# Base rows by channel batches, C and B by DMA, planes normalised in phase order, in a four-layer convolution kernel

## The chip, the cores and the metric

One core of a Trainium2 chip runs the whole program. The metric is the device time of one execution in microseconds (us), here as the median of several. PE, DVE, ACT and POOL are the compute engines; SP issues most DMAs. Work passes between engines by semaphores.

## What is computed

Four layers follow one another on x of shape 2 x 192 x 64 x 64; before each one the channels are normalised in groups of six, and its result is added to its input.

```python
# layer 0
base = conv1x1(x, w_qkv)                                    # 576 channels
qkv = concat(dw3x3(base), dw5x5(base), dw7x7(base))         # 1728 channels
qkv = conv1x1(qkv, w_pconv)                                 # channel attention on q, k, v, top-k softmax, w_proj
# layer 1: q, k, v = conv1x1(x, w_qkv); softmax(q k^T) v over channels, 8 heads
# layer 2: scan over 4096 positions, 192 channels, 16 states n
h = exp(d_t * A) * h + (d_t * x_t) * B_t[n]
y_t = sum_n h[n] * C_t[n] + x_t * D                         # then W_out
# layer 3: depthwise 7 x 7 convolution and a bias
```

## The kernel before

Channels lie on partitions in `NT` = 3 tiles: tile 0 and 1 hold channels 0 to 127 of either image, tile 2 holds channels 128 to 191 of both, 64 partitions each (`pieces`). `mem` is the one SBUF arena, `ps` the one PSUM tensor, so these names stand in nearly every row of the profile.

**Layer 0, depthwise.** `layer0_depthwise` has 36 batches n of 16 base channels. The rows of an image are sorted by phase: 56 rows (`TAPROWS`) on partitions, so that a depthwise convolution becomes matmuls with tap matrices. The 1x1 product gives the base for 128 channels m at a time, in eight groups g; ACT and DVE split it into high and low fp16 parts (`base`), POOL shifts six groups by a column (`shift`), and SP stores both to `base_phases` in DRAM (`store_base` L405, `store_shifted` L413). m = 0 is done ahead; m + 1 is done in the first four batches of each eight, two groups a batch. For a batch, SP loads windows from `base_phases` (`load_windows` L425, two DMAs, to partitions 0 to 55 and 64 to 119) and taps from `in_wd` (`load_taps` L399, also two). ACT copies the taps to fp16 (`taps`, L535, L538), POOL takes the low part (`split_taps`, L579, L582), PE runs four units of 36 matmuls (L500), each copied out by ACT (L545) and split by DVE (L606), and SP stores the 96 rows (`store_out` L431, three DMAs of 32 partitions). SP's order in a batch is: outputs of n - 1, windows of n + 2, taps of n + 2, base stores. There are three window buffers and two tap buffers.

**Layer 2.** `layer2` first makes delta, B and C by products; B and C in three bf16 parts are moved between partitions by 24 SBUF-to-SBUF DMAs. The scan then runs for t in three tiles, j in four chunks of 1024 positions, n in 16 states, 192 steps in all. For a step: PE spreads row B[n] over the partitions with a selector matmul (`b_bcast`, L1526), ACT makes the decay (L1593), DVE multiplies (L1665) and scans (L1679), PE spreads C[n] to PSUM (`c_bcast`, L1535), ACT copies it to `cs` (L1599), POOL multiplies h by it (L1650), PE adds over states (`accumulate`, L1551). For the four `POOL_STATES` the B row goes by PE (L1542) and ACT (L1602) to POOL, which makes the product (L1647) in place of DVE. ACT also keeps the last column of h (L1579).

**Layer 3.** `layer3` normalises each tile, splits it into fp16 high and low parts in phase order, mirrors columns and rows at the borders, and stores planes to DRAM, 4 MB for tile 0 and 1 and twice 2 MB for tile 2. ACT makes the high part from the natural layout (L1854), DVE the normalised tile (L1924) and the low part (L1928) and the columns (L1931, L1932); POOL makes two shifted copies (L1894, L1895) and the low part of the taps (L1888); then DVE copies the mirrored rows (`rows(t)`, L1912, L1914), which SP's store (L1794) waits for. Then 12 steps load patches (L1808, four DMAs), multiply (L1841), copy out (ACT L1872) and store to `conv_d` (L1876); SP loads the sums back by channel (L1818), DVE adds (L1946), SP stores the result (L1822).

## Time and profile before

| | us |
|---|---|
| median of 3 runs | 2782.25 |
| lowest and highest | 2777.99, 2783.22 |
| the profiled execution | 2779.78 |
| its span, first to last instruction | 2777.9 |

| stretch, us | work |
|---|---|
| 94 to 627 | batches of layer 0's depthwise part |
| 1731 to 2476 | the 192 scan steps of layer 2 |
| 2542 to 2778 | layer 3 after its norm |

Times in rows are us unless marked ns. The DMA share is the busy share of the core's 16 DMA engines. A transfer that is issued waits behind those issued earlier on its queue.

### The profile page before, as it was taken

Reading aid. Unit: us, or ns where it says so; the run is one execution under the profiler, and the core shown is the slowest. Engines: PE = TensorE matmul, PEld = TensorE weight load, DVE = VectorE, ACT = ScalarE, POOL = GpSimd, SP = SyncE. Lnnn points to the kernel's source line nnn. Section 1 sums busy time; section 2 is a strip of 40 time slices with the busy share of each in tenths; the row PEclk is TensorE's granted clock in tenths of the full one; section 3 lists DMA queues with packets and bytes.
Section 4 is the critical chain, followed back from the end, with each engine's and each line's share of the span. In section 5 each row is a group of like instructions: output and inputs, shape, how many; then the busy total and the mean of one; then the engine's idle time right before and its main releaser. Section 6 shows DMA issues by size and latency. Waiting matters only on the chain. (4 is left out here: it accounts for less than half of the span.)

```text
span 2777.9 us, 38167 instructions
## 1 busy us (share of the span) xinstructions
PE 2059.9 (74%) x16032; PEld 1257.4 (45%) x16032; DVE 1303.1 (47%) x1197; ACT 1022.2 (37%) x1444; POOL 849.1 (31%) x446
## 2 busy tenths in 40 slices
PE   3768787767999999999489658777678678772032
PEld 1466665665777777777235222222223223221021
DVE  5334344341011010111450265798889799979703
ACT  2344444440000000000132236667676766655110
POOL 1333323220000000000000120687688678873300
PEclk9989898878999999999699779899899899996555
DMA  5899999987331331310300041000000000013399
GB/s 167 256 270 279 247 309 233 271 228 210 93 107 57 104 107 54 107 54 1 96 3 7 7 134 23 0 0 0 0 1 0 0 0 0 0 50 93 142 226 279
DMA packets 157448, 292.93 MB, mean 105 GB/s; under 512 B 10284, under 2 KB 135212, under 8 KB 151084
## 3 DMA queue, kind: packets, MB, share of 16 engines
q1 hardware_dynamic: 144620, 284.39, 36.1%
q10 hardware_dynamic: 12672, 6.29, 0.8%
q8 instruction: 118, 1.93, 0.3%
q14 instruction: 38, 0.31, 0.0%
HBM read 168.16 MB, written 120.91 MB: 104 GB/s over the span
## 5 line engine op out<-in xcount | busy, mean ns | idle before, releaser
L675 PE MATMUL ps<-mem 128*128 128x288 f16 x5376 | 653.9, 287 | 19.5 <-DMA mem<-depthwise_out 19.5
L675 PEld LDWEIGHTS ps<-mem 128*128 128x128 f16 x5376 | 501.8, 98 | 157.5 <-DMA mem<-depthwise_out 19.7
L1650 POOL TENSOR_TENSOR mem<-mem 128x1024 f32<-128x1024 f32 x192 | 460.6, 2412 | 86.1 <-ACT mem L1579 85.7
L1551 PE MATMUL ps<-mem 128*128 128x512 f32 x768 | 388.2, 630 | 12.9 <-POOL mem L1650 12.1
L500 PE MATMUL ps<-mem 56*96 56x240 f16 (+1 forms) x5184 | 311.8, 282 | 107.6 <-DVE mem L606 98.3
L1679 DVE TENSOR_TENSOR_SCAN mem<-mem,ps 128x1024 f32<-128x1024 f32 x144 | 335.8, 2332 | 89.7 <-issue 50.7
L500 PEld LDWEIGHTS ps<-mem 56*96 56x96 f16 x5184 | 300.5, 130 | 133.9 <-DVE mem L606 106.0
L1072 POOL TENSOR_TENSOR mem<-mem 128x1536 f16<-128x1536 f32 x16 | 50.8, 3179 | 996.3 <-ACT mem L1052 996.3
L715 DVE TENSOR_TENSOR mem<-mem 128x384 f32<-128x384 f32 x64 | 35.7, 559 | 610.8 <-ACT mem L729 610.8
L606 DVE TENSOR_TENSOR mem<-ps,mem 96x1024 f16<-96x1024 f32 x144 | 171.2, 1216 | 225.2 <-ACT mem L545 224.0
L727 ACT COPY mem<-ps 128x288 f32<-128x288 f32 x64 | 25.5, 398 | 645.7 <-PE ps L675 645.7
L1599 ACT COPY mem<-ps 128x1024 f32<-128x1024 f32 x192 | 194.1, 1011 | 121.3 <-PE ps L1535 78.4
L1551 PEld LDWEIGHTS ps<-mem 128*128 128x128 f32 x768 | 148.3, 199 | 160.0 <-issue 102.3
L545 ACT CAST mem<-ps 96x1024 f16<-96x1024 f32 x144 | 140.1, 1007 | 103.9 <-PE ps L500 103.9
L1526 PE MATMUL ps<-mem 96*128 (+1 forms) x288 | 91.1, 405 | 117.1 <-DVE mem L1679 110.1
L1665 DVE TENSOR_TENSOR ps<-ps,mem 128x1024 f32<-128x1024 f32 x144 | 174.2, 1209 | 2.4 <-PE ps L1526 2.4
L1647 POOL TENSOR_TENSOR mem<-mem 128x1024 f32<-128x1024 f32 x48 | 115.7, 2410 | 165.4 <-ACT mem L1602 165.3
L1593 ACT ACTIVATE mem<-mem 128x1024 f32<-128x1024 f32 (+1 forms) x144 | 165.5, 1150 | 1.4 <-issue 1.1
L579 POOL TENSOR_TENSOR mem<-mem 120x768 f16<-120x768 f32 x36 | 62.0, 1722 | 326.9 <-ACT mem L538 326.9
L1841 PE MATMUL ps<-mem 56*32 56x256 f16 x1728 | 43.9, 378 | 157.6 <-DMA mem<-l_planes 127.3
L1535 PE MATMUL ps<-mem 96*128 (+1 forms) x384 | 120.2, 396 | 53.3 <-ACT mem L1602 53.3
L481 PE MATMUL ps<-mem 128*128 128x512 f32 (+1 forms) x160 | 92.4, 707 | 43.2 <-DVE mem L600 26.7
(204 smaller groups left out, 2119.0 us busy)
## 6 DMA issues: line engine op xcount, KB each, us to landing
depthwise_out<-mem SPq DMA_DIRECT2D x108, 512.0 KB, 8.1
mem<-depthwise_out SPq DMA_DIRECT2D x32, 1664.0 KB, 9.9
mem<-base_phases SPq DMA_DIRECT2D x72, 448.0 KB
base_phases<-mem SPq DMA_DIRECT2D x56, 512.0 KB, 9.6
mem<-in_wd SPq DMA_DIRECT2D x72, 336.0 KB
mem<-l_planes SPq DMA_DIRECT2D x48, 252.0 KB
mem<-in_x SPq DMA_DIRECT2D x4, 2048.0 KB, 11.0
l_planes<-mem SPq DMA_DIRECT2D x2, 4032.0 KB, 13.3
```

Of the source, the lines that this page charges most:

```text
L500: ins = nc.tensor.matmul(out.rearrange("p (b n) -> p b n", b=B)[:, :, lo:hi], wh[n % 2][p, c0:c0 + MD], x, start=(o == 1 and i == 0), stop ...
L545: nc.scalar.copy(stg_part(n, k, 0), dw_psum(u)).then_inc(dw_hi, 1)
L606: nc.vector.tensor_tensor(stg_part(n, k, 1), dw_psum(u), stg_part(n, k, 0), ALU.subtract).then_inc(dw_lo, 1)
L675: ins = nc.tensor.matmul(ps[:, 2 * (i % 2) + h, 0:HALF], d, pw[rows, wa, k, HALF * h:HALF * h + HALF], start=(k == 0 and n == 0), stop=(k ...
L1535: ins = nc.tensor.matmul(pc[:, a, :], sel[0:96, N * t + n, :], bc3[0:96, 1, bass.ds(j * CH + 512 * a, 512)], start=True, stop=True)
L1551: ins = nc.tensor.matmul(py[:, a, :], ident, hh[:, n % 4, 512 * a:512 * a + 512], start=(n % N == 0), stop=(n % N == N - 1))
L1593: nc.scalar.activation(decay, halves(zs[t][:, bass.ds(j * CH, CH)]), ACT.Exp, scale=na[:, t, n:n + 1]).then_inc(exp_done, 1)
L1599: nc.scalar.copy(halves(cs[:, n % 2, :]), pc).then_inc(c_copied, 1)
L1647: nc.gpsimd.tensor_tensor(dbx, dbx, dxs[t % 2][:, bass.ds(j * CH, CH)], ALU.mult).then_inc(dbx_pool, 1)
L1650: nc.gpsimd.tensor_tensor(hh[:, n % 4, :], hh[:, n % 4, :], cs[:, n % 2, :], ALU.mult).then_inc(hc_pool, 1)
L1665: V.tensor_tensor(pb[n % 2], pb[n % 2], halves(dxs[t % 2][:, bass.ds(j * CH, CH)]), ALU.mult).then_inc(dbx_done, 1)
L1679: V.tensor_tensor_scan(hh[:, n % 4, :], decay, drive, 0.0 if first else hs[:, n:n + 1], ALU.mult, ALU.add).then_inc(scan_done, 1)
```

## The change

**Layer 0.** `base_phases` in DRAM is laid out by phase row, then channel, where it was channel, then row. A window load then reads 8 KB in one run for each partition (eight neighbouring channels) where it read eight runs of 1 KB (every other channel); a base store writes four runs of 1 KB for each partition where it wrote one of 4 KB. `stg_part` and the tap layout follow the new pairing of channels. There are three tap buffers, `load_taps` runs three batches ahead, and ACT converts the taps of n + 1 after unit 1 of batch n, where it did so ahead of unit 0.

```diff
-        base_d = nc.dram_tensor("base_phases", [QKV, TAPROWS, PITCH0], F16).ap()
+        base_d = nc.dram_tensor("base_phases", [TAPROWS, QKV, PITCH0], F16).ap()
...
-    NM, NSTB, NWIN, NSTG = 5, 4, 3, 3
-    w = ar.take(2, QKV)
+    NM, NSTB, NWIN, NSTG, NTB = 5, 4, 3, 3, 3
+    w = spare.rearrange("p a c -> p (a c)").rearrange("p (a c) -> p a c", a=2)
...
-    w32 = [ar.take(BP * TAPS0) for _ in range(2)]
+    w32 = [ar.take(BP * TAPS0) for _ in range(NTB)]
...
 
-        return stg[n % NSTG][0:MD, 4 * k:4 * k + 4, 256 * a:256 * a + 256].rearrange("p (q t) n -> p t q n", t=2)
...
-                    sp.dma_start(base_d[128 * m:128 * m + width(m), row:row + 4, :].rearrange("c r n -> c (r n)"),
-                                 ext[0:width(m), SHIFTED.index(g)].rearrange("p r n -> p (r n)")).then_inc(ext_stored[SHIFTED.index(g)], 16)
+                    sp.dma_start(base_d[row:row + 4, 128 * m:128 * m + width(m)].rearrange("r c n -> c r n"),
+                                 ext[0:width(m), SHIFTED.index(g)]).then_inc(ext_stored[SHIFTED.index(g)], 16)
...
-                    sp.dma_start(win[64 * t:64 * t + TAPROWS, slot], base_d[c0 + t:c0 + 2 * BP:2].rearrange("c f n -> f c n")
-                                 ).then_inc(win_loaded[slot], 16)
+                    sp.dma_start(win[64 * t:64 * t + TAPROWS, slot], base_d[:, c0 + BP * t:c0 + BP * t + BP]).then_inc(win_loaded[slot], 16)
...
@@ -452,9 +451,10 @@
                     if (n + 2) % BP == 0:
                         wait_stored((n + 2) // BP)
                     load_windows(n + 2)
+                if n + NTB < NBATCH:
                     sp.wait_ge(w_lo, NTAP * (n + 1))
                     sp.wait_ge(w_hi, NTAP * (n + 1))
-                    load_taps(n + 2)
+                    load_taps(n + NTB)
...
-                if n + 1 < NBATCH:
-                    taps(n + 1)
                 for k in range(UPB):
                     for m, g in base_before(n, k):
                         base(m, g)
                     unit(n, k)
+                    if k == 1 and n + 1 < NBATCH:
+                        taps(n + 1)
```

ACT in two batches that make no base; L545 is a unit's copy, L535 and L538 are the taps of the next batch. Before:

```order
L535 CAST mem<-mem 120x8x96 [waits l0_depthwise_in_psum_54,l0_taps_loaded_48]
L538 CAST mem<-mem 120x8x2x8
L538 CAST mem<-mem 120x8x2x16
L538 CAST mem<-mem 120x8x2x24
L545 CAST mem<-ps 96x2x2x256 [waits l0_depthwise_stored_58,l0_depthwise_in_psum_54]
L545 CAST mem<-ps 96x2x2x256 [waits l0_depthwise_in_psum_54] x3
```

Now:

```order
L545 CAST mem<-ps 96x2x2x256 [waits l0_depthwise_stored_59,l0_depthwise_in_psum_55]
L545 CAST mem<-ps 96x2x2x256 [waits l0_depthwise_in_psum_55]
L535 CAST mem<-mem 120x8x96 [waits l0_depthwise_in_psum_55,l0_taps_loaded_49]
L538 CAST mem<-mem 120x8x2x8
L538 CAST mem<-mem 120x8x2x16
L538 CAST mem<-mem 120x8x2x24
L545 CAST mem<-ps 96x2x2x256 [waits l0_depthwise_in_psum_55] x2
```

The four conversions stand behind two units of a batch, and the unit copies of the same batch that stood behind them are ahead.

**Layer 2.** B and C are stored in fp32 to DRAM (`bc_d`) during the products, and half of the SBUF moves go. For each step SP loads the row C[n] from there into one of four slots of `cs`, as two DMAs that each repeat one 4 KB row on 64 partitions; for a state of `POOL_STATES` it does the same for B into one of two slots of `dbx`. PE's `c_bcast` and `pool_b_bcast` and ACT's two copies are gone. The products split B and C through a new tile, so that the unsplit values can be stored.

```diff
+            for k in range(NK2):
+                sp.wait_ge(bc_out, k + 1)
+                for b in range(B):
+                    sp.dma_start(bc_d[b, :, 512 * k:512 * k + 512], full[64 * b:64 * b + 2 * N_STATE, k % 2]).then_inc(bc_stored[k % 2], 16)
+                if k % 4 == 3:
+                    s = slice(512 * (k - 3), 512 * (k + 1))
+                    sp.wait_ge(bcv, 5 * (k + 1))
+                    for part in range(3):
+                        for b in range(B):
+                            sp.dma_start(b3[32 * part + 16 * b:32 * part + 16 * b + 16, s],
+                                         parts[64 * b:64 * b + 16, part, s]).then_inc(moved, 16)
...
+                for h in range(2):
+                    b = t if t < 2 else h
+                    sp.dma_start(dst[64 * h:64 * h + 64], bc_d[b, row, j * CH:j * CH + CH].partition_broadcast(64)).then_inc(done, 16)
+
+            def load_b(m):
+                t, j, n = m // (N * NCH), m // N % NCH, m % N
+                if pool_count(t, j, n) > 2:
+                    sp.wait_ge(scan_done, m - 8 + 3)
+                spread(dbx[:, pool_slot(n)], n, t, j, b_loaded[pool_slot(n)])
+
+            load_b(POOL_STATES[0])
+            for m in range(N * NCH * NT):
+                t, j, n = m // (N * NCH), m // N % NCH, m % N
+                if m + 4 < N * NCH * NT and (m + 4) % N in POOL_STATES:
+                    load_b(m + 4)
+                if m >= 4:
+                    sp.wait_ge(hc_pool, m - 4 + N + 1)
+                spread(cs[:, n % 4], N + n, t, j, c_loaded[n % 4])
+
         @block.tensor
         def _(pe):
             def b_bcast(t, j, n):
                 pe.wait_ge(scan_done, count(t, j, n) + 1)
...
-            def c_bcast(t, j, n):
-                pe.wait_ge(c_copied, count(t, j, n) + 1)
-                if n - 1 in [q - 2 for q in POOL_STATES]:
-                    pe.wait_ge(b_copied, pool_count(t, j, n + 1))
-                for a in range(2):
-                    ins = nc.tensor.matmul(pc[:, a, :], sel[0:96, N * t + n, :], bc3[0:96, 1, bass.ds(j * CH + 512 * a, 512)],
-                                           start=True, stop=True)
-                ins.then_inc(csum, 1)
...
-                    c_bcast(t, j, n)
                     if n >= 2 or not first:
                         accumulate(t, j, n - 2)
-                    if n + 2 in POOL_STATES:
-                        pool_b_bcast(t, j, n + 2)
...
-                    act.wait_ge(csum, count(t, j, n) + 1)
-                    wait_times_c(act, t, j, n - 2)
-                    nc.scalar.copy(halves(cs[:, n % 2, :]), pc).then_inc(c_copied, 1)
-                    if n + 2 in POOL_STATES:
-                        act.wait_ge(bsum_pool, pool_count(t, j, n + 2))
-                        nc.scalar.copy(halves(dbx), pc).then_inc(b_copied, 1)
...
-                            pool.wait_ge(b_copied, pool_count(t, j, n + 2))
-                            nc.gpsimd.tensor_tensor(dbx, dbx, dxs[t % 2][:, bass.ds(j * CH, CH)], ALU.mult).then_inc(dbx_pool, 1)
+                            db = dbx[:, pool_slot(n + 2)]
+                            pool.wait_ge(b_loaded[pool_slot(n + 2)], 32 * ((pool_count(t, j, n + 2) + 1) // 2))
+                            nc.gpsimd.tensor_tensor(db, db, dxs[t % 2][:, bass.ds(j * CH, CH)], ALU.mult).then_inc(dbx_pool, 1)
                         pool.wait_ge(carried, m + 3)
-                        pool.wait_ge(c_copied, m + 2)
-                        nc.gpsimd.tensor_tensor(hh[:, n % 4, :], hh[:, n % 4, :], cs[:, n % 2, :], ALU.mult).then_inc(hc_pool, 1)
+                        pool.wait_ge(c_loaded[n % 4], 32 * (m // 4 + 1))
+                        nc.gpsimd.tensor_tensor(hh[:, n % 4, :], hh[:, n % 4, :], cs[:, n % 4, :], ALU.mult).then_inc(hc_pool, 1)
```

ACT in the first chunk of a scan; L1593 (now L1606) is the decay, L1579 (L1592) the kept column, L1583 (L1596) the skip term. Before:

```order
L1593 ACTIVATE mem<-mem 128x1024 [waits l2_scan_120]
L1579 COPY mem<-mem 128x1 [waits l2_scan_120]
L1599 COPY mem<-ps 128x1024 [waits l2_h_times_c_121,l2_c_broadcast_114]
L1602 COPY mem<-ps 128x1024 [waits l2_pool_b_broadcast_118]
L1583 ACTIVATE mem<-mem 128x2048 [waits l2_dx_ready_111]
L1593 ACTIVATE mem<-mem 128x1024 [waits l2_scan_120]
L1579 COPY mem<-mem 128x1 [waits l2_scan_120]
```

Now:

```order
L1606 ACTIVATE mem<-mem 128x1024 [waits l2_scan_126]
L1592 COPY mem<-mem 128x1 [waits l2_scan_126]
L1596 ACTIVATE mem<-mem 128x2048 [waits l2_dx_ready_114]
L1606 ACTIVATE mem<-mem 128x1024 [waits l2_scan_126]
L1592 COPY mem<-mem 128x1 [waits l2_scan_126]
```

The copies L1599 and L1602 between the decays are gone.

**Layer 3.** ACT alone normalises, a quarter r at a time, into `tmp` in phase order; DVE copies that to the high part and subtracts it for the low part. One shifted copy moves from POOL to ACT, the other to DVE, and `rows(t)` follows its own tile's columns. The first taps load during the norm. `stg` has four slots and shares memory with `tmp`. The result is added and stored in halves. Some semaphores are layer 0's again, with their counts as a base.

```diff
-            for i in range(NPIECE):
-                if i >= 2:
-                    sp.wait_ge(tap_hi, i - 1)
-                    sp.wait_ge(tap_lo, i - 1)
-                sp.dma_start(w32[i % 2][0:64 + TAPROWS], inp["wd3"][:, 3 * WC * i:3 * WC * (i + 1)]).then_inc(tap_in[i % 2], 16)
             for t in range(NT):
+                if t < 2:
+                    sp.wait_ge(tap_hi, t + 1)
+                    sp.wait_ge(tap_lo, t + 1)
+                    load_taps(sp, t + 2)
                 sp.wait_ge(rows_done, t + 1)
...
+            for k in range(NSTG):
+                sp.wait_ge(conv_stored[k], 32 * (128 // CB // NSTG))
             sp.wait_ge(stored[2], 32)
...
+                for h in range(2):
+                    s = slice(HW // 2 * h, HW // 2 * (h + 1))
+                    sp.wait_ge(added, 8 * t + 4 * h + 4)
+                    for p0, b, c0, n in pieces(t):
+                        sp.dma_start(xout[b, c0:c0 + n, s], xt[p0:p0 + n, t, s]).then_inc(out_stored, 16)
...
+            def normalise(t):
                 for r in range(4):
-                    nc.scalar.activation(flat(main_rows(t, r, 0)), natural(xt[:, t], r), ACT.Identity,
-                                         bias=nb[:, t:t + 1], scale=rs[:, t:t + 1]).then_inc(x_hi, 1)
+                    if t:
+                        act.wait_ge(x_lo, 4 * t - 3 + r)
+                    nc.scalar.activation(phase_rows(r).rearrange("p f (y x) -> p f y x", x=8), natural(xt[:, t], r), ACT.Identity,
+                                         bias=nb[:, t:t + 1], scale=rs[:, t:t + 1]).then_inc(x_norm, 1)
...
-            split(0)
+            def shift_right(t):
+                k = t % 2
+                act.wait_ge(x_lo, 4 * (t + 1))
+                nc.scalar.copy(grid(pl[:, k, 8:11])[:, :, :, 1:8], grid(pl[:, k, 5:8])[:, :, :, 0:7]).then_inc(shifted, 1)
+
+            normalise(0)
             taps(0)
-            split(1)
-            taps(1)
-            split(2)
-            taps(2)
-            taps(3)
+            for t in range(NT):
+                shift_right(t)
+                if t + 1 < NT:
+                    normalise(t + 1)
+                taps(t + 1)
...
+                if n >= NSTG:
+                    act.wait_ge(conv_stored[n % NSTG], 32 * (n // NSTG))
...
-            for t in range(NT):
-                pool.wait_ge(x_lo, 4 * (t + 1))
-                pool.wait_ge(x_hi, 4 * (t + 1))
-                k = t % 2
-                nc.gpsimd.tensor_copy(grid(pl[:, k, 8:11])[:, :, :, 1:8], grid(pl[:, k, 5:8])[:, :, :, 0:7]).then_inc(shifted, 1)
-                nc.gpsimd.tensor_copy(grid(pl[:, k, 11:14])[:, :, :, 0:7], grid(pl[:, k, 0:3])[:, :, :, 1:8]).then_inc(shifted, 1)
-                taps(t)
-            taps(3)
+            for i in range(NPIECE):
+                taps(i)
...
+                if t == 2:
+                    dve.wait_ge(stored[0], 16)
                 for r in range(4):
+                    dve.wait_ge(x_norm, 4 * t + r + 1)
+                    V.tensor_copy(main_rows(t, r, 0), phase_rows(r)).then_inc(x_hi, 1)
                     dve.wait_ge(x_hi, 4 * t + r + 1)
-                    V.tensor_tensor(flat(main_rows(t, r, 1)), natural(tmp, r), flat(main_rows(t, r, 0)), ALU.subtract).then_inc(x_lo, 1)
+                    V.tensor_tensor(main_rows(t, r, 1), phase_rows(r), main_rows(t, r, 0), ALU.subtract).then_inc(x_lo, 1)
                 dve.wait_ge(x_lo, 4 * t + 4)
+                V.tensor_copy(grid(pl[:, k, 11:14])[:, :, :, 0:7], grid(pl[:, k, 0:3])[:, :, :, 1:8]).then_inc(shifted, 1)
                 for i in range(3):
                     V.tensor_copy(column(k, 8 + i, 0), column(k, 3 - i, 0)).then_inc(columns, 1)
                     V.tensor_copy(column(k, 11 + i, 7), column(k, 6 - i, 7)).then_inc(columns, 1)
-                if t:
-                    rows(t - 1)
-            rows(NT - 1)
+                rows(t)
...
+                dve.wait_ge(conv_in[t], conv_base[t] + 16 * len(pieces(t)))
+                for h in range(2):
+                    for r in range(4):
+                        x = natural(xt[:, t], r)[:, :, 8 * h:8 * h + 8]
```

DVE in layer 3 where the second tile ends. L1912 and L1914 before are the rows of the first tile, and L1924, L1928 the third tile. Before:

```order
L1932 COPY mem<-mem 128x8x16
L1912 COPY mem<-mem 128x14x2x8 x3
L1914 COPY mem<-mem 128x14x2x8 x3
L1924 TENSOR_SCALAR mem<-mem 128x4096
L1928 TENSOR_TENSOR mem<-mem 128x8x128 x4
L1931 COPY mem<-mem 128x8x16
```

Now (L1955, L1956 are columns, L1935 and L1937 rows, L1953 the shifted copy, L1949 and L1951 the high and low part), where the first tile ends and the second begins:

```order
L1955 COPY mem<-mem 128x8x16
L1956 COPY mem<-mem 128x8x16
L1935 COPY mem<-mem 128x14x2x8 x3
L1937 COPY mem<-mem 128x14x2x8 x3
L1949 CAST mem<-mem 128x8x128
L1951 TENSOR_TENSOR mem<-mem 128x8x128
```

The rows of a tile stand right behind its columns, where they stood behind the whole next tile.

## Rows read from the trace of the kernel before

**Rows 1.** Stretches (from:to, length, busy us of each engine, clock, DMA share, GB/s).

```profile
94.00:627.00 533.00, 409.74 (x5424) 330.85 (x5422) 217.33 (x207) 234.04 (x343) 160.51 (x159) 0.88 0.96 263
```

**Rows 2.** Waits of 90 to 650 us: who for whom, total us, times, longest.

```profile
ACT mem L535 <- DMA mem<-in_wd: 161.4, 33, 10.9
...
PE ps L500 <- DVE mem L606: 98.3, 21, 9.7
```

**Rows 3.** Stretches in which one kind of transfer moves almost alone.

```profile
4.00:12.00 8.00, 0.00 (x0) 0.00 (x0) 2.84 (x5) 0.00 (x0) 0.00 (x0) 1.00 1.01 430
13.00:21.00 8.00, 0.00 (x0) 0.00 (x0) 5.85 (x10) 0.00 (x0) 0.00 (x0) 1.00 0.95 199
574.00:578.00 4.00, 4.00 (x77) 4.00 (x79) 1.22 (x1) 0.67 (x1) 0.00 (x0) 1.00 0.94 199
...
1605.00:1608.00 3.00, 3.00 (x22) 1.06 (x22) 2.17 (x4) 0.16 (x1) 2.76 (x1) 1.00 0.96 367
...
2502.00:2504.00 2.00, 0.94 (x4) 0.42 (x5) 2.00 (x2) 0.40 (x1) 0.96 (x1) 0.96 0.96 246
```

**Rows 4.** DMA of 735 to 740 us, 1 KB packets to 128 partitions.

```profile
DMA packets 1714, 1.71 MB, mean 341 GB/s; under 512 B 48, under 2 KB 1714, under 8 KB 1714
```

**Rows 5.** DMA issues of the page: count, KB of one, us to landing.

```profile
mem<-base_phases SPq DMA_DIRECT2D x72, 448.0 KB
base_phases<-mem SPq DMA_DIRECT2D x56, 512.0 KB, 9.6
...
mem<-l_planes SPq DMA_DIRECT2D x48, 252.0 KB
```

**Rows 6.** Groups of instructions, 1731 to 2476 us: busy us, mean ns, idle before, releasers.

```profile
L1650 POOL TENSOR_TENSOR mem<-mem 128x1024 f32<-128x1024 f32 x192 | 460.6, 2412 | 86.1 <-ACT mem L1579 85.7
L1551 PE MATMUL ps<-mem 128*128 128x512 f32 x768 | 388.2, 630 | 12.9 <-POOL mem L1650 12.1 <-DVE mem L1684 0.6
L1679 DVE TENSOR_TENSOR_SCAN mem<-mem,ps 128x1024 f32<-128x1024 f32 x144 | 335.8, 2332 | 89.7 <-issue 50.7 <-ACT mem L1593 19.5 <-DVE ps L1665 17.3
L1599 ACT COPY mem<-ps 128x1024 f32<-128x1024 f32 x192 | 194.1, 1011 | 121.3 <-PE ps L1535 78.4 <-POOL mem L1650 42.8
L1665 DVE TENSOR_TENSOR ps<-ps,mem 128x1024 f32<-128x1024 f32 x144 | 174.2, 1209 | 2.4 <-PE ps L1526 2.4
...
L1647 POOL TENSOR_TENSOR mem<-mem 128x1024 f32<-128x1024 f32 x48 | 115.7, 2410 | 165.4 <-ACT mem L1602 165.3
```

**Rows 7.** Timeline at one state of `POOL_STATES`: start, us, engine, line.

```profile
2015.12 1.01 ACT L1602 COPY mem<-ps 128x1024 f32<-128x1024 f32 x1 [1.14 <-PE ps L1542]
...
2016.03 1.15 ACT L1593 ACTIVATE mem<-mem 128x1024 f32<-128x1024 f32 x1
...
2017.27 2.29 DVE L1679 TENSOR_TENSOR_SCAN mem<-mem,ps 128x1024 f32<-128x1024 f32 x1 [0.86 <-DVE ps L1665]
```

**Rows 8.** Stretches: the scans as a whole, and their first 60 us.

```profile
1731.00:2476.00 745.00, 564.34 (x1535) 213.38 (x1532) 647.39 (x359) 508.38 (x652) 574.75 (x240) 0.94 0.00 0
1731.00:1791.00 60.00, 41.13 (x99) 15.16 (x96) 43.59 (x25) 42.05 (x49) 35.18 (x15) 0.79 0.00 0
```

**Rows 9.** Timeline of layer 3, in order of time.

```profile
2558.81 4.60 DVE L1932 COPY mem<-mem 128x128 f16<-128x128 f16 x1
...
2585.16 44.20 SPq L1794 DMA_DIRECT2D l_planes<-mem  x4
2600.67 8.58 ACT L1854 ACTIVATE mem<-mem 128x1024 f16<-128x1024 f32 x4 [36.89 <-DMA l_planes<-mem]
...
2626.96 0.47 DVE L1914 COPY mem<-mem 128x224 f16<-128x224 f16 x3
...
2637.87 84.52 SPq L1808 DMA_DIRECT2D mem<-l_planes  x48
...
2663.93 3.95 PE L1841 MATMUL ps<-mem 56*32 56x256 f16 x144 [125.16 <-DMA mem<-l_planes]
```

**Rows 10.** Waits of 2530 to 2778 us.

```profile
ACT mem L1872 <- DMA l_conv<-mem: 13.7, 2, 8.4
```

145 lines of the change are left out of this document (66 added, 79 removed).

## The prediction

> **What bounds the kernel now.** I read the busy shares by stretch first, since the three changed places have different limits, then in each stretch what is waited for.
>
> In layer 0's depthwise part, 94 to 627 us, the DMA engines are busy for 0.96 of 533 us and PE for 410 us [rows 1]. ACT waits 161 us in total for taps, and PE 98 us for a PSUM bank that frees late, behind ACT [rows 2]. That looks like a stall to be removed, but while ACT waits, the DMA engines are moving the bytes it waits for: only the 0.04 left, 21 us, is idle DMA time. So transfers set this stretch. What a transfer costs depends on the partitions it touches: 128 partitions go at 430 GB/s, and 64 partitions, in the same kind of load, at 199; 56 partitions in 1 KB runs (the windows) at 199 too; 4 KB runs are stored from tiles of mostly 128 partitions at 367 [rows 3]. 1 KB runs to 128 partitions go at 341 [rows 4].
>
> In the scans, 1731 to 2476 us, nearly no DMA runs. DVE is busy for 647 of 745 us, POOL 575, PE 564, ACT 508 [rows 8]. DVE's idle time stands almost wholly before the scans, 89.7 us [rows 6]. One place shows why: ACT copies B from PSUM (L1602) from 2015.12 on, so its decay (L1593), which starts at 2016.03, ends only at 2017.18, and DVE's scan starts at 2017.27, 0.86 us late [rows 7]; the row names DVE as the releaser, but its product had ended. In the first 60 us DVE is busy for only 43.6 [rows 8]. DVE is the bound, and ACT's copies are what makes it late.
>
> In layer 3 a chain of preparations ends in the stores of the planes and the patch loads behind them. The third tile's high part starts at 2600.67, after the first store has landed, and the rows of the second and third tile follow only at the end, up to 2627.4 (three copies of 0.47 us in the row); the patch loads are issued at 2637.87 and PE starts at 2663.93, after 125 us of waiting for patches [rows 9].
>
> **Layer 0, part by part.** Windows: 72 loads of 448 KB [rows 5], 0.92 MB a batch. At the 199 GB/s of the row they take 4.6 us, and as runs of 8 KB they still go to 56 partitions, so I take half of 430, 215 GB/s, 4.3 us: 36 x 0.34 = 12 us less DMA time. Bounds: nothing, and 36 x 2.5 = 89 us less at 430, which I exclude because large runs to 64 partitions stayed at 199. Base stores: 56 of 512 KB [rows 5] and 14 of half that, 63 units. A unit takes 1.43 us at 367 GB/s and 1.54 at 341, so +0.11 each, 7 us; the other bound is the windows' own 199, 2.63 us, +76 us. I take the near one, +9 with some margin, since these stores use 128 partitions. Taps three ahead and converted mid-batch move the same bytes, one batch's earlier; they could give back the 21 us of idle DMA time. Against it: POOL now splits the taps mid-batch, and its shifts of the base rows, queued behind, come later, and SP's store of the shifted rows, and behind that the outputs of the next batch, wait for them. I take 5 us back. How late are the taps of n + 1? In all, a batch costs ACT 234 / 36 = 6.5 us, with four unit copies and its share of the base, and POOL 160.5 / 36 = 4.5, with the shifts [rows 1]; so I put the conversion at some 2 us and the split under 4.5, together 6 after unit 1, while PE's other two units take half of its 410 / 36 = 11.4, 5.7 us with base products among them, 4 without. PE would wait up to 2 us a batch, which hides while the DMAs set a batch at 533 / 36 = 14.8 us, and costs if they stop doing so. Sum for layer 0: -12 + 9 - 5 = -8 us, bounds -35 and +65.
>
> **Layer 2, part by part.** PE loses the 384 matmuls of `c_bcast` and the 96 for POOL's B, ACT loses 192 copies of 1.011 us [rows 6] and 48 more, 243 us of its 508. The decays can then run as far ahead as the PSUM bank and the scan two steps back let them, so I let the waits before scans go by two thirds: 0.65 x 89.7 = 58 us. Not more, because POOL is near: four steps cost it 5 x 2.41 = 12.1 us, and DVE 3 x (2.33 + 1.21) + 2.3 = 12.9 [rows 6]. The new transfers: four steps need ten DMAs of 256 KB, 2.6 MB. Every one touches 64 partitions: at 246 GB/s (4 KB runs, half of the partitions [rows 3]) that is 10.7 us, at 199 it is 13.2 us, which would set the pace. I take up to 12, between them and nearer to the first, whose runs are of the same 4 KB: just hidden beneath DVE's 12.9, with four slots of C, about 13 us, to cover a late one. No row shows one DRAM row read 64 times over; its bounds are these rates and a rival below. SP issues some 480 DMAs and does nothing else here. If the cover is gone, each 1 us more for four steps costs 48 us. The stores of B and C and the 12 moves fewer lie beside the products; costed at nothing. Bounds for the scans: -78 and -20 (POOL and the transfers in turn late), catastrophes apart.
>
> The Trainium skill, "DMA: Bandwidth & Descriptors", section "Anatomy of one DMA — SWDGE (gpsimd) path", fits 2.0 us plus bytes / 436 GB/s for a single DMA (of another queue than SP's). By that, one after the other, ten DMAs of 256 KB take 26 us for four steps, and the scans 48 x 26 = 1250 us. The sum by the rule would be 1250 - 687 = 563 us slower than mine. The row speaks against it: 48 patch loads of 252 KB are issued in 84.5 us, 1.8 us each with conv stores among them [rows 5, 9], so queued DMAs overlap their fixed part. I go by the row; what it leaves of the rule is rival F.
>
> **Layer 3, part by part.** ACT's quarter takes 8.58 / 4 = 2.15 us [rows 9] as before. DVE's pair in place of normalising and subtracting I put at 0.9 + 1.2 us: the second is the 1209 ns of the same size in [rows 6], the first, an unseen cast, lies between 0.5 and 1.2. So a tile takes some 9 us, then the shifted copy some 2, six columns at 0.47, 3, and the rows 1. A DVE copy beside POOL's tap subtraction waits it out (4.60 us for one small copy, where others take 0.47, [rows 9]); I add that once a tile. From 2542 to the store of tile 0 are thus 20 us: 2563, and then 2583 and 2603. Before, the first was at 2585.16 and the last after 2627.4 [rows 9]. The first store has landed by 2575, ahead of the third tile's need. Patch loads then stand only behind tile 2's 4 MB from 64 partitions, 19 us at half rate, and not behind tile 1's as well: 2663.9 becomes about 2631, -32 us. Bounds -22 and -38. The twelve steps stay at their DMA pace. At the end ACT waits 13.7 us for stores of its two stage slots [rows 10], queued against SP's loads; with four slots the last sums are stored earlier and tile 2's load follows: -6 us, bounds 0 and -12. Halved adds save little, as the outputs wait for each other on the DMA engines.
>
> **Sum.** -8 - 58 - 32 - 6 = -104 us. The profiled execution took 2779.8, so 2675.8; it lies inside the three runs, 2.5 us under their median, and I leave the forecast at 2676.
>
> **Rivals.**
>
> A, slower: the repeated row. All 16 DMA engines read the same 4 KB 64 times, then again for the other half. If that halves the rate of 246 GB/s to 123, four steps take 21.3 us, the scans 48 x 21.3 = 1022 us and the whole 2676 + 335 = 3011. It decides from the rate at which four steps take more than 745 / 48 + 46 / 48 = 16.5 us, 159 GB/s, where all that the other parts gain is eaten. For it: no row shows such a load. Against it: nothing in the rows slows with the source, only with the partitions reached. Chance 0.08.
>
> The Trainium skill, "SBUF — State Buffer", section "A bandwidth-pool intuition that's wrong (but worth ruling out)", gives about 22.5 GB/s for one of 32 HBM ports. Were a 4 KB row behind one port, four steps would take 116 us and the scans over 5 ms; no run here shows how rows spread, and this is the far end of A.
>
> B: the scans are paced by POOL and the transfers together, 15.1 us for four steps (12.1 of POOL and 3 of waiting for loads): scans 725 us, total 2676 + 38 = 2714. For it: 12.1, 12 and 12.9 us are close. Chance 0.14.
>
> C: the base stores in 1 KB runs go at the windows' rate: +76 in place of +9, total 2743. For it: they share engines with windows. Against it: 341 GB/s with 128 partitions. Chance 0.07.
>
> D: the taps were more than a symptom: with bigger runs and earlier taps PE's waits of 98 us [rows 2] halve as well, 41 us more than I gave, with the stretch down to 484 us, total 2676 - 41 = 2635. For it: transfers that PE's waits delay would go with them. Against it: 0.96 of 533 us is 512 us of DMA work, which would have to shrink by more than the 12. Chance 0.13.
>
> E: PE's clock. Less PE work in the scans; in their first 60 us PE was busy for 41 and the granted clock 0.79 against 0.94 over all [rows 8], between 1.2 and 2.4 GHz. If it stayed low, `accumulate`, four times 0.63 us at mostly full clock [rows 6], and B would pass DVE's 3.5 us a step; the scans 100 us longer than now forecast, the total 2776, within 0.2% of before. Chance 0.03.
>
> F: transfers that cost what the patch loads cost, 84.5 / 48 = 1.76 us for 252 KB [rows 5, 9], whatever the reason. Ten take 17.6 us for four steps, the scans 845 us, 158 more than forecast, total 2834. It decides above the same 16.5 us as A. For it: the size is the same. Against it: conv stores from few partitions share those 84.5 us. Chance 0.02.
>
> The forecast itself has 0.53.
>
> **How the numbers follow.** The forecast's own spread runs from 2640 to 2710. B adds up to 2714 to 2730, D down to 2630. The range 2628 to 2735 leaves out A, E, F, C's upper half and the ends of D, 0.2 together. A measurement can tell 0.2%, 5.6 us. Faster by more: forecast, B, C, D, 0.87, less 0.01 for their ends. Within: part of E, 0.02. Slower: A, F and the worse half of E, 0.12.
>
> **What would show it.** In the profile after: DMA share near 0.97 in layer 0 and a stretch of 515 to 540 us; ACT no longer waiting for taps at the head of a batch. In the scans a DMA share around 0.8 to 0.95, the idle time before scans under 35 us, ACT under 300 us busy, POOL's waits on loads small. In layer 3 the first store of planes 21 us after the start of the stage (2563 against 2542, where it was 43), all three within 42 us, and 27 to 30 us from the last to PE's start. It is wrong if POOL waits long for the loads of C (A or B), if the base stores' windows show under 300 GB/s (C), or if layer 0 is shorter by over 30 us (D).

## The result, and the profile after

| | before | after |
|---|---|---|
| median, us | 2782.73 | 2617.67 |
| lowest and highest | 2777.99, 2785.88 | 2613.45, 2630.39 |
| profiled execution, span | 2779.78, 2777.9 | 2617.27, 2615.5 |

The ratio is 0.9416, with a 95% interval of 0.9381 to 0.9451: 165 us less, where 104 was forecast and the range's lower end was 2628. By stage, from the two traces:

| stage | before | after | difference | forecast |
|---|---|---|---|---|
| layer 0, first to last depthwise matmul | 534.0 | 471.2 | -62.8 | -8 |
| layer 2, first to last scan | 736.0 | 672.2 | -63.8 | -58 |
| layer 3, last scan to the end | 307.8 | 272.0 | -35.8 | -38 |
| all else | 1200.1 | 1200.1 | 0.0 | 0 |

Two of the three terms held. Layer 0 gave 55 us more than it was priced at, and the excess of the total over the forecast, 58 us, is nearly all there.

Three stretches of after (columns as in [rows 1]): layer 0's batches, four of them with base products, and the scans.

```profile
92.00:563.00 471.00, 393.86 (x5432) 324.31 (x5428) 222.08 (x207) 239.93 (x348) 162.11 (x164) 0.92 0.96 297
...
410.00:450.00 40.00, 40.00 (x480) 26.15 (x476) 22.33 (x24) 23.32 (x36) 17.05 (x16) 1.00 0.98 294
1671.00:2344.00 673.00, 492.97 (x1047) 186.24 (x1048) 642.54 (x357) 281.08 (x409) 575.74 (x240) 0.87 0.74 186
```

The first row answers to [rows 1]: the DMA share is 0.96 as before, but the same bytes now go at 297 GB/s where they went at 263, and PE's busy time of 394 us fills 84% of the stage in place of 77%. In the second row PE is busy for 40.00 of 40 us while the DMA share is 0.98: a share near one stands beside a PE that never waits. The third row answers to [rows 8]: DVE is busy for 643 of 673 us, ACT for 281 where it had 508, the DMA share is 0.74, and the granted clock has gone from 0.94 to 0.87.

Waits of after, 88 to 580 us (as [rows 2]):

```profile
PE ps L500 <- DMA mem<-base_phases: 59.4, 9, 11.3
...
PE ps L500 <- DVE mem L606: 10.2, 3, 6.7
```

ACT's 161 us for taps are gone from this list, and PE's 98 us for a bank that DVE frees (L606) are 10. What is left is 59 us for windows.

Groups of after in the scans (as [rows 6]):

```profile
L1687 DVE TENSOR_TENSOR_SCAN mem<-mem,ps 128x1024 f32<-128x1024 f32 x144 | 335.8, 2332 | 26.6 <-issue 9.0 <-ACT mem L1606 8.7 <-ACT ps L1606 3.5
L1673 DVE TENSOR_TENSOR ps<-ps,mem 128x1024 f32<-128x1024 f32 x144 | 174.1, 1209 | 3.4 <-PE ps L1558 3.3
```

DVE's idle time before its scans is 26.6 us in place of 89.7. Its own instructions take what they took, 2332 and 1209 ns. With 643 of 673 us busy, DVE has little left to give back.

Timeline of after in layer 3 (as [rows 9]):

```profile
2416.50 8.64 ACT L1882 ACTIVATE mem<-mem 128x1024 f32<-128x1024 f32 x4 [1.93 <-PEq L203]
...
2435.44 0.35 SPq L1822 DMA_DIRECT2D l_planes<-mem  x1
...
2451.17 22.77 SPq L1822 DMA_DIRECT2D l_planes<-mem  x3
...
2474.12 91.50 SPq L1836 DMA_DIRECT2D mem<-l_planes  x48
...
2501.45 3.83 PE L1871 MATMUL ps<-mem 56*32 56x256 f16 x136 [88.12 <-DMA mem<-l_planes]
```

ACT starts to normalise at 2416.50, and the first store of planes is issued 19 us later, at 2435.44; the last is issued before 2474.12, when the patch loads begin, and PE starts 27 us after that. The forecast had 20 or 21 us, and 27 to 30.

### The profile page after: what moved, and what is told of

The parts are those of the page before. It is cut to its first block and busy times, and to the rows that moved or that the text cites. A ratio compares the mean times of both kernels' runs of the same rounds, so it can differ in the third digit from the quotient of the medians.

```text
span 2615.5 us, 37175 instructions
## 1 busy us (share of the span) xinstructions
PE 1977.8 (76%) x15552; PEld 1225.0 (47%) x15552; DVE 1291.3 (49%) x1222; ACT 808.9 (31%) x1207; POOL 835.6 (32%) x440
## 5 line engine op out<-in xcount | busy, mean ns | idle before, releaser
L1567 PE MATMUL ps<-mem 128*128 128x512 f32 x768 | 429.6, 691 | 23.3 <-POOL mem L1658 19.0
L1687 DVE TENSOR_TENSOR_SCAN mem<-mem,ps 128x1024 f32<-128x1024 f32 x144 | 335.8, 2332 | 26.6 <-issue 9.0
L606 DVE TENSOR_TENSOR mem<-ps,mem 96x1024 f16<-96x1024 f32 x144 | 175.4, 1220 | 219.2 <-ACT mem L545 219.2
L1567 PEld LDWEIGHTS ps<-mem 128*128 128x128 f32 x768 | 163.5, 221 | 222.0 <-issue 127.0
L1558 PE MATMUL ps<-mem 96*128 (+1 forms) x288 | 99.5, 436 | 162.6 <-DVE mem L1687 160.0
L545 ACT CAST mem<-ps 96x1024 f16<-96x1024 f32 x144 | 144.9, 1008 | 191.0 <-PE ps L500 191.0
L1673 DVE TENSOR_TENSOR ps<-ps,mem 128x1024 f32<-128x1024 f32 x144 | 174.1, 1209 | 3.4 <-PE ps L1558 3.3
L1606 ACT ACTIVATE mem<-mem 128x1024 f32<-128x1024 f32 (+1 forms) x144 | 163.5, 1143 | 1.3 <-issue 1.0
L1592 ACT COPY mem<-mem 128x1 f32<-128x1 f32 x192 | 36.6, 191 | 390.4 <-DVE mem L1687 390.4
L1558 PEld LDWEIGHTS ps<-mem 96*128 96x128 bf16 x288 | 23.8, 105 | 273.6 <-DVE mem L1687 234.9
L1687 DVE TENSOR_TENSOR_SCAN mem<-ps,mem 128x1024 f32<-128x1024 f32 x48 | 111.1, 2314 | 0.0
```

Source lines behind the costliest of these rows:

```text
L545: nc.scalar.copy(stg_part(n, k, 0), dw_psum(u)).then_inc(dw_hi, 1)
L606: nc.vector.tensor_tensor(stg_part(n, k, 1), dw_psum(u), stg_part(n, k, 0), ALU.subtract).then_inc(dw_lo, 1)
L1558: ins = nc.tensor.matmul(pb[n % 2][:, a, :], sel[0:96, N * t + n, :], b3[0:96, bass.ds(j * CH + 512 * a, 512)], start=True, stop=True)
L1567: ins = nc.tensor.matmul(py[:, a, :], ident, hh[:, n % 4, 512 * a:512 * a + 512], start=(n % N == 0), stop=(n % N == N - 1))
L1606: nc.scalar.activation(decay, halves(zs[t][:, bass.ds(j * CH, CH)]), ACT.Exp, scale=na[:, t, n:n + 1]).then_inc(exp_done, 1)
L1673: V.tensor_tensor(pb[n % 2], pb[n % 2], halves(dxs[t % 2][:, bass.ds(j * CH, CH)]), ALU.mult).then_inc(dbx_done, 1)
```

## The experiments

Each edit is made to the changed kernel, if not said otherwise. "Stage" is layer 0 from the first to the last depthwise matmul. Eight profiles in which layer 0's code is that of the change have stages of 471 to 482 us, and where the scans' code is untouched too they take 670 to 672 us; so differences of up to 11 us count as nothing in layer 0, and of 2 in the scans.

| run | edit | median, us | ratio | stage | scans |
|---|---|---|---|---|---|
| the change | | 2617.7 | 0.942 | 471 | 672 |
| `e1_old_taps` | two tap buffers, conversion ahead of unit 0 | 2671.2 | 0.959 | 530 | 672 |
| `e2_old_rows` | old row layout | 2617.8 | 0.941 | 470 | 672 |
| `e3_head` | three buffers, conversion ahead of unit 0 | 2606.6 | 0.936 | 463 | 672 |
| `e4_two_buffers` | two buffers, conversion mid-batch | 2649.2 | 0.950 | 510 | 672 |
| `e5_taps_first` | `e1_old_taps`, taps first in SP's order | 2586.0 | 0.928 | 447 | 670 |
| `b1_before_first` | the kernel before, taps first | 2690.8 | 0.966 | 437 | 733 |
| `o6_first_old_rows` | `e5_taps_first`, old row layout | 2585.5 | 0.929 | 443 | 670 |
| `o7_first_three` | the same, three buffers | 2586.5 | 0.929 | 448 | 672 |
| `o2_spread_base` | base steps over six batches | 2613.7 | 0.939 | 474 | 672 |
| `o1_two_queues` | upper partitions on ACT's queue | 2638.0 | 0.947 | 498 | 672 |
| `c1_more_bytes` | `e3_head`, 344 KB more a batch | 2650.9 | 0.952 | 501 | 672 |
| `s1_all_partitions` | loads of C and B to 128 partitions | 2619.3 | 0.941 | 476 | 672 |
| `s2_act_copies` | one more ACT copy a step | 2627.5 | 0.943 | 473 | 679 |
| `s4_copies_that_wait` | and it waits for POOL | 2627.3 | 0.943 | 476 | 682 |
| `s5_both_and_wait` | and a second copy, for 48 states | 2629.6 | 0.944 | 474 | 686 |
| `s6_c_by_pe` | C by PE and ACT again | 2652.1 | | 477 | 707 |
| `s7_b_by_pe` | POOL's B by PE and ACT again | 2680.3 | | 473 | 738 |
| `l3_both` | rows a tile later, two stage slots | 2632.1 | | 482 | 672 |

Where no ratio stands there was one execution, and only its trace is read.

### Layer 0: layout or timing of the taps

Edit of `e1_old_taps`:

```diff
-    NM, NSTB, NWIN, NSTG, NTB = 5, 4, 3, 3, 3
+    NM, NSTB, NWIN, NSTG, NTB = 5, 4, 3, 3, 2
...
+                if n + 1 < NBATCH:
+                    taps(n + 1)
                 for k in range(UPB):
...
-                    if k == 1 and n + 1 < NBATCH:
-                        taps(n + 1)
```

> The changed kernel with layer 0's taps as before: two tap buffers, loads two batches ahead, ACT converting the taps of n + 1 ahead of unit 0. The new row layout stays. In the changed kernel layer 0's stage (first to last depthwise matmul) takes 471 us, against 534 before. Theory 'rows' (the 8 KB window runs alone bring the gain): 471 to 480 us, total 2618 to 2627. Theory 'timing' (the taps' timing brings most of the 63 us): 505 to 525 us, total 2650 to 2670. If both carry a share, some 490, total 2637.

The stage is 530 us: the timing of the taps carries 59 of the 63. The stretch and two waits of this run:

```profile
92.00:622.00 530.00, 414.11 (x5432) 336.26 (x5432) 218.16 (x207) 234.60 (x343) 158.73 (x159) 0.88 0.94 265
```

```profile
ACT mem L535 <- DMA mem<-in_wd: 155.9, 33, 10.0
...
PE ps L500 <- DVE mem L606: 95.4, 18, 9.4
```

Both waits are those of before, 161 and 98 us, within 6 us. The new layout alone moved the stage from 534 to 530, less than the 11 us by which it varies.

Edit of `e2_old_rows` (and the base stores accordingly):

```diff
-        base_d = nc.dram_tensor("base_phases", [TAPROWS, QKV, PITCH0], F16).ap()
+        base_d = nc.dram_tensor("base_phases", [QKV, TAPROWS, PITCH0], F16).ap()
...
-                    sp.dma_start(win[64 * t:64 * t + TAPROWS, slot], base_d[:, c0 + BP * t:c0 + BP * t + BP]).then_inc(win_loaded[slot], 16)
+                    sp.dma_start(win[64 * t:64 * t + TAPROWS, slot], base_d[c0 + BP * t:c0 + BP * t + BP].rearrange("c f n -> f c n")).then_inc(win_loaded[slot], 16)
```

> The changed kernel with base_phases by channel, then row, as before: windows in 1 KB runs, base stores in 4 KB runs; three tap buffers and mid-batch conversion stay. Theory 'rows': layer 0 at 520 to 535 us, total 2667 to 2680. Theory 'timing': 475 to 490 us, total 2622 to 2637. If each carries a share alone, the two deficits of this run and of the one with old taps add up to 63 us; if either needs the other, they add up to more.

Stage and total are those of the change. So no run shows a worth of the layout, with late taps (4 us) or with taps in time (0). The two deficits, 59 and 0, add up to 63 but for what the stage varies by.

### Which half of the timing

`e3_head` puts the conversion back ahead of unit 0 and keeps three buffers; `e4_two_buffers` has two buffers and keeps the conversion mid-batch: the two halves of the first diff above.

> The changed kernel with three tap buffers and loads three batches ahead, but ACT converts the taps of n + 1 ahead of unit 0 of batch n, as before. With both the depth and the place of before, layer 0's stage took 530 us; with both changed, 471. Theory 'late transfer' (the taps arrive late because their load could not be issued earlier): depth alone brings it, stage 471 to 485 us, total 2618 to 2632. Theory 'place' (ACT's wait stands ahead of unit copies that could go): 515 to 530 us, total 2660 to 2675.

> The changed kernel with two tap buffers and loads two batches ahead, as before, but ACT converting the taps of n + 1 after unit 1 of batch n. Theory 'place': stage 471 to 485 us, total 2618 to 2632. Theory 'late transfer': 515 to 530 us, total 2660 to 2675. If each alone does nearly all, both runs stand near 2620: half a batch of slack in either form would have been enough.

The third buffer alone does all of it. It stands 8 us below both together (463 us against 471), which the stage's variation could make; the totals, 2606.6 and 2617.7, point the same way, with ratio intervals that just touch (up to 0.9387, from 0.9381). The place alone gives 20 of the 59. Mid-batch conversion seems to cost something beside three buffers, since PE then waits for the late split: 18.7 us for POOL (L582) in the trace of after, a wait that `e3_head` doesn't show. The prediction had feared up to 2 us a batch for it.

### Why the taps were late

Edit of `e5_taps_first`, on top of `e1_old_taps`:

```diff
             for n in range(NBATCH):
+                if n + NTB < NBATCH:
+                    sp.wait_ge(w_lo, NTAP * (n + 1))
+                    sp.wait_ge(w_hi, NTAP * (n + 1))
+                    load_taps(n + NTB)
                 if n >= 1:
                     store_out(n - 1)
...
                     load_windows(n + 2)
-                if n + NTB < NBATCH:
-                    sp.wait_ge(w_lo, NTAP * (n + 1))
-                    sp.wait_ge(w_hi, NTAP * (n + 1))
-                    load_taps(n + NTB)
```

> The changed kernel with layer 0's taps as before (two buffers, conversion ahead of unit 0, stage 530 us in that form), but SP issues the load of the taps of n + 2 first in batch n, ahead of its wait for the outputs of n - 1 and of the windows, where it stood behind both. Same bytes. Theory 'round trip' (the taps are late because their load stands behind the outputs' and windows' transfers in SP's order, and ACT's wait for them then holds up the next outputs): stage 465 to 490 us, total 2608 to 2630. Rival 'amount' (transfers as a whole set the stage with two buffers, in any order): 520 to 535 us, total 2660 to 2675.

Two buffers, the old place of the conversion, the same bytes, and only four lines of SP's program moved: 447 us, less than with the change's three buffers. The load was late since SP issued it behind `store_out(n - 1)`, which waits until the whole batch n - 1 is computed, and behind the outputs and windows themselves, 2.5 MB a batch. The edit takes it out from behind both; which of the two weighs more was not separated. The same edit in the kernel before:

> The kernel before, with one edit: SP issues layer 0's load of the taps of n + 2 first in batch n, ahead of the stores of outputs n - 1 and the windows. Theory 'round trip' (the late taps, not the bytes, set the stage): the stage falls from 534 us to 445 to 480, total 2695 to 2730. Rival (the gain of the run with the taps first needed the new layout or the new later stages): 515 to 534 us, total over 2765.

The stage falls from 534 to 437 us, the total to 2690.8, a ratio of 0.966 with an interval of 0.964 to 0.969. One moved load gives 97 us, more than all that the change does to layer 0. SP's own wait for outputs shrinks with it, to 12.2 us in 7 waits; in the kernel before, over the stage, it is:

```profile
SPq L431 <- DVE mem L606: 132.2, 34, 9.6
```

The round trip can be read in the kernel before, around batch 15 (timeline: start, us, engine, line; in brackets the idle time before and who ended it):

```profile
306.70 2.96 SPq L431 DMA_DIRECT2D depthwise_out<-mem  x3
...
310.03 3.95 SPq L425 DMA_DIRECT2D mem<-base_phases  x2
...
314.08 1.04 SPq L399 DMA_DIRECT2D mem<-in_wd  x2
...
324.12 0.83 ACT L535 CAST mem<-mem 120x768 f16<-120x768 f32 x1 [9.26 <-DMA mem<-in_wd]
...
325.78 2.81 ACT L545 CAST mem<-ps 96x1024 f16<-96x1024 f32 x3
...
328.09 3.91 PE L500 MATMUL ps<-mem 56*96 56x256 f16 x36 [8.61 <-DVE mem L606]
```

The outputs of n - 1 are stored at 306.70, as soon as they exist, windows follow at 310.03 and taps at 314.08. These taps land ten microseconds later, at 324.1, where ACT has waited 9.26 us for them; three finished units stand behind that wait in ACT's order, so PE waits 8.61 us for a bank. And the next outputs, the next loads behind them, and so the next taps, start later by as much. In the same kernel with the taps first:

```profile
310.64 2.64 SPq L399 DMA_DIRECT2D mem<-in_wd  x2
...
313.33 3.10 SPq L431 DMA_DIRECT2D depthwise_out<-mem  x3
...
316.48 4.86 SPq L425 DMA_DIRECT2D mem<-base_phases  x2
...
320.41 0.83 ACT L536 CAST mem<-mem 120x768 f16<-120x768 f32 x1
...
322.27 3.94 PE L501 MATMUL ps<-mem 56*96 56x256 f16 x72
```

Here the taps (310.64) go ahead of the outputs (313.33) and windows (316.48), and ACT converts taps at 320.41 without a wait. The two stretches are not quite alike: here the batches also make base products, so that PE has more to do while the loads run. In batches without base this run has waits for taps too (5.87 us at 253.30); over the stage there are 15 of them, where there were 33. The stretch and the waits of this run:

```profile
94.00:531.00 437.00, 385.73 (x5432) 315.01 (x5430) 220.33 (x207) 237.67 (x344) 162.42 (x159) 0.95 0.99 322
```

```profile
ACT mem L536 <- DMA mem<-in_wd: 45.7, 15, 9.0
...
PE ps L501 <- DVE mem L607: 32.6, 12, 6.1
```

The share is 0.99, higher than before, and the rate is 322 GB/s where it was 263, with packets of the same sizes: counted in the two traces over these stretches, a 16 KB packet of an output store takes 904 ns on average before and 749 here, a 6 KB packet of taps 394 and 308, a 1 KB packet of windows 74 and 61, and a 4 KB packet of a base store 169 and 170. The traces give a hint why. Before, 42% of the window packets ran while at least nine in ten packets under way were of their own size, and took 77 ns each; here 11% do, at the same 77 ns. But the others fell as well, from 72 to 59 ns, so this is not all of it. The wait for taps is 46 us in place of 161.

### What bounds layer 0 now

Edit of `c1_more_bytes`, on top of `e3_head`:

```diff
+                if n:
+                    sp.wait_ge(win_loaded[(n - 1) % NWIN], 64 * ((n - 1) // NWIN + 1))
+                for t in range(2):
+                    sp.dma_start(more[64 * t:64 * t + TAPROWS], base_d[:, c0:c0 + 3]).then_inc(win_loaded[slot], 16)
```

> The kernel with three tap buffers and the conversion at the head (stage 463 us, total 2607), with 344 KB more to load in each of the 36 batches, from base_phases in 3 KB runs to the windows' partitions, into a place that nobody reads; PE waits for it as for the windows. At the windows' 199 GB/s this is 1.7 us a batch, 62 us in all. Theory 'transfers set the stage' (their share is 0.97): 510 to 530 us. Rival 'PE sets it' (most batches take PE's own 13.5 or 10.5 us): 463 to 475 us. Between the two: only the batches that wait for windows grow, 480 to 500 us.

```profile
94.00:595.00 501.00, 405.93 (x5432) 333.45 (x5428) 220.92 (x207) 238.80 (x344) 164.90 (x159) 0.89 0.97 303
```

```profile
SPq L430 <- DMA mem<-base_phases: 72.4, 17, 14.4
```

The second row is SP's wait for the windows and added loads of the batch before, which the edit brings with it. The stage is 501 us, 38 more, about 0.6 of the 62 us that the bytes were priced at: with 12 MB more and a share of 0.97 again, the rate is 303 GB/s, as it was 301 without them. That doesn't show that the amount counts, though. SP stands 72.4 us in the added wait, which `e3_head` doesn't have, with the taps and the outputs behind it in SP's order. Bytes and lateness are not told apart by this run, and what bounds the stage of 471 us stays open: PE fills 84% of it and waits 59 us for windows. The share alone says the same in all these runs.

> The changed kernel with the base steps of a block of 16 batches' channels spread over six batches of each eight (two, one, one, two, one, one groups), where two groups were made in each of the first four. In the changed kernel the batches with base run at 13.5 us and those without at 10.5, which is PE's own pace, but the fifth and sixth of each eight take 15 to 18 us, waiting for windows that stand behind the base stores. If that queue is the cause, spreading the stores saves 4 to 10 us in each of the four eights: the stage 440 to 458 us, total 2587 to 2605. Rival (total transfer time sets the stage, share 0.96): 468 to 475 us, total within 4 us of 2618.

The stage is 474 us and the total 2613.7: nothing (the edit is `for k < 6` with groups (0, 1), (2), (3), (4, 5), (6), (7) in `base_steps`). The wait for windows moved to other batches; the expectation was also wrong in that 10.5 us is PE's own pace without base: in `e5_taps_first`, some batches without base take 7.5.

Edit of `o1_two_queues` in ACT's program, behind unit (n, 0); SP's part of the same three loops is taken out:

```diff
+                    act.dma_start(d_dram[:, 2 * QKV + 2 * BP * (n - 1):2 * QKV + 2 * BP * n], stg[(n - 1) % NSTG][PHASES * 2:PHASES * 3]
...
+                    act.dma_start(win[64:64 + TAPROWS, (n + 2) % NWIN], base_d[:, c0 + BP:c0 + 2 * BP]).then_inc(win_loaded[(n + 2) % NWIN], 16)
...
+                    act.dma_start(w32[q % NTB][64:64 + TAPROWS], inp["wd"][TAPROWS:2 * TAPROWS, q * BP * TAPS0:(q + 1) * BP * TAPS0]
```

> The changed kernel with layer 0's transfers of partitions 64 and up (one output store of three, one window load and one tap load of two) issued by ACT on its own queue, behind its first unit of a batch; SP keeps those of partitions 0 to 63. Same bytes and packets. Theory 'halves' (a transfer that reaches only half of the partitions runs at half rate unless one of the other half runs beside it, 199 against 430 GB/s): packets get shorter, DMA share of the stage falls under 0.9, the stage falls from 471 to 415 to 440 us and PE sets it; total 2562 to 2587. Rival (a packet costs what it costs, whatever runs beside it): 468 to 475 us and total 2615 to 2622, or up to 15 us slower because ACT's issues and its wait for DVE delay its copies.

The stage is 498 us, 27 longer. A batch of it on ACT and its queue:

```profile
302.59 1.01 ACT L545 CAST mem<-ps 96x1024 f16<-96x1024 f32 x1 [5.68 <-PE ps L500]
302.60 0.31 ACTq L550 DMA_DIRECT2D depthwise_out<-mem  x1
302.95 1.10 ACTq L560 DMA_DIRECT2D mem<-base_phases  x1
...
304.09 2.06 ACTq L564 DMA_DIRECT2D mem<-in_wd  x1
306.19 1.01 ACT L545 CAST mem<-ps 96x1024 f16<-96x1024 f32 x1 [2.59 <-PE ps L500]
```

The three issues keep ACT's queue for 3.5 us (302.60 to 306.15), and the second unit copy starts right behind them, at 306.19, with the conversion behind it; the share is 0.94. That this lateness makes the 27 us is read from such batches and not tested by itself. Neither theory's number came. Whether transfers to the two halves of the partitions gain from running side by side can't be told from this run, as ACT's lateness covers it. That stays open.

### The first rows and buffers again, with the taps first

> The changed kernel's later layers with layer 0 as in the kernel before, row layout included, but with the load of the taps first in SP's order (two buffers, conversion ahead of unit 0). With the new layout this order gave a stage of 447 us and a total of 2586; in the kernel before it gave 437. Theory 'the new rows cost or bring nothing once PE is near its own pace': 436 to 448 us, total 2575 to 2588. Rival (the 8 KB runs help here too): over 455 us, total over 2592.

> As the run with the taps first and the old rows, with three tap buffers. If taps that are issued first still come late now and then, the stage falls below the other's by 3 to 10 us. Rival (a batch's slack is enough, and loads issued still earlier push the windows back behind them): the same within 4 us, or up to 10 us slower.

The stages are 443 and 448 us, the totals 2585.5 and 2586.5: neither the layout nor the third buffer has a value of its own once the load is issued early. These and `e5_taps_first` are the fastest kernels of the study, a ratio of 0.929 (intervals from 0.925 to 0.933) to the kernel before.

### Layer 2: the new loads

Edit of `s1_all_partitions`:

```diff
                 for h in range(2):
-                    b = t if t < 2 else h
-                    sp.dma_start(dst[64 * h:64 * h + 64], bc_d[b, row, j * CH:j * CH + CH].partition_broadcast(64)).then_inc(done, 16)
+                    if t < 2:
+                        sp.dma_start(dst[:, CH // 2 * h:CH // 2 * h + CH // 2],
+                                     bc_d[t, row, j * CH + CH // 2 * h:j * CH + CH // 2 * h + CH // 2].partition_broadcast(128)).then_inc(done, 16)
+                    else:
+                        sp.dma_start(dst[64 * h:64 * h + 64], bc_d[h, row, j * CH:j * CH + CH].partition_broadcast(64)).then_inc(done, 16)
```

> The changed kernel with the scans' loads for the first two channel tiles cut another way: each of the two DMAs repeats half a row (2 KB) on all 128 partitions, where it repeated a whole row (4 KB) on 64. The third tile is as it was. Theory 'halves': the DMA share in the first two tiles' scans falls from about 0.73 to 0.4 to 0.5, the third tile's stays; the time stays within 5 us of 2618, because DVE is busy for 645 of 672 us and sets the pace. Rival A (the source row is the limit): the share stays near 0.73 in all three tiles. Rival B (transfers still pace the scans): the total falls by 10 us or more.

Second and third tile, first of the change, then of this run:

```profile
1890.00:2110.00 220.00, 161.79 (x344) 61.40 (x345) 209.77 (x118) 94.94 (x136) 187.37 (x79) 0.87 0.73 185
2120.00:2340.00 220.00, 165.62 (x358) 62.29 (x358) 213.93 (x121) 84.18 (x133) 191.76 (x81) 0.89 0.75 189
```

```profile
1890.00:2110.00 220.00, 161.85 (x347) 61.21 (x348) 210.35 (x119) 94.95 (x136) 187.91 (x79) 0.88 0.58 186
2120.00:2340.00 220.00, 166.39 (x360) 62.72 (x359) 213.89 (x121) 84.08 (x132) 193.07 (x82) 0.89 0.76 188
```

The share of the second tile falls from 0.73 to 0.58 and that of the third stays; the rate stays too, 185 to 189 GB/s, since DVE asks for so much and no more. While busy, the loads thus go at 185 / 0.73 = 253 GB/s on 64 partitions, beside the 246 that the prediction took from [rows 3], and at 186 / 0.58 = 321 on 128. The Trainium skill, "SBUF — State Buffer", section "Door 1: The DMA port swizzle (why `[64,N]` ≈ `[32,N]`)", says that a transfer's rate goes by the ports that its partitions reach; this trace agrees in direction, with a factor of 1.27 rather than two; the packets on 128 partitions are half as long, 2 KB, and no run here has 4 KB ones on 128. The scans take the same time: transfers don't pace them. Rivals A, B and F are out with that.

### Layer 2: what had made the scans late

Edit of `s5_both_and_wait` in ACT's program; `s4_copies_that_wait` is without its last two lines, and `s2_act_copies` without the wait for POOL (`wait_times_c`) as well:

```diff
                         keep_state(t, j, n - 1)
+                    act.wait_ge(carried, count(t, j, n) * 2 + 1 + 4 * (j + NCH * t) + seconds(n - 1))
+                    wait_times_c(act, t, j, n - 2)
+                    nc.scalar.copy(spare, zs[t][:, 0:CH]).then_inc(carried, 1)
+                    if n + 2 in POOL_STATES:
+                        nc.scalar.copy(ps[:, 4:6, :], halves(zs[t][:, 0:CH])).then_inc(carried, 1)
```

> The changed kernel with one more ACT copy of 128 x 1024 in each of the 192 scan steps, behind the kept column, into a place that nobody reads: the time of ACT's copy of C before, without its PSUM and its waits. The output is unchanged. Theory 'ACT's copies made the scans late': ACT's busy time rises by some 190 us and the idle time before scans from 27 to 60 to 90 us, scans 672 to 700 to 735 us, total 2650 to 2680. Rival (the gain came from PE's and the PSUM bank's share of the C and B chain, or from the waits between engines, not from ACT's time): scans within 8 us of 672.

> The changed kernel with one more ACT copy of 128 x 1024 in each scan step, as in the run with ACT copies, but each now also waits for POOL's product with C two steps back, as ACT's copy of C did before because it had two slots. With the copies alone the scans took 679 us, without them 672, before 736. Theory 'ACT waits for POOL': 700 to 736 us, total 2645 to 2682. Rival (POOL's step two back is done by then anyway): 676 to 685 us.

> As the run whose copies wait for POOL, and with a second copy of 128 x 1024 to PSUM two steps ahead of each state of POOL_STATES, where ACT copied B for POOL before. ACT then has the time of before, some 508 us busy, and its wait for POOL, but no wait for PE's spread of C or B. Theory 'ACT's order': scans 715 to 740 us, total 2660 to 2685. Rival (ACT's waits for PE's C and B in PSUM carry the rest): under 705 us.

The scans take 679, 682 and 686 us: with ACT's time of before given back in full, and its wait for POOL, the scans lose 14 of the 64 us. Groups of the last of the three:

```profile
L1697 DVE TENSOR_TENSOR_SCAN mem<-mem,ps 128x1024 f32<-128x1024 f32 x144 | 335.8, 2332 | 42.5 <-issue 18.7 <-DVE ps L1683 15.4 <-ACT mem L1611 5.5
L1617 ACT CAST mem<-mem 128x1024 bf16<-128x1024 f32 x192 | 200.2, 1043 | 10.7 <-POOL mem L1668 7.5
```

So it was not ACT's time alone. That leaves what ACT waited for, PE: in the kernel before 78.4 us for the spread of C ([rows 6]) and this for B:

```profile
ACT mem L1602 <- PE ps L1542: 54.1, 48, 3.0
```


Edit of `s6_c_by_pe` in SP's, PE's and ACT's program; `s7_b_by_pe` does the like for POOL's B:

```diff
-                spread(cs[:, n % 4], N + n, t, j, c_loaded[n % 4])
...
+                    c_bcast(t, j, n)
...
+                    act.wait_ge(csum, count(t, j, n) + 1)
+                    wait_times_c(act, t, j, n - 2)
+                    nc.scalar.copy(halves(cs[:, n % 2, :]), ps[:, 4:6, :]).then_inc(c_copied, 1)
```

> The changed kernel with C brought as before: PE spreads the row to PSUM, ACT copies it to one of two slots, POOL multiplies; B for POOL stays on the DMA. The spread takes B's rows for C's (the split C is no longer moved), so the values differ and the work is the same. Scans now 672 us, before 736; ACT's time and its wait for POOL alone gave 686. Theory 'PE in ACT's order' (the decay of the next state stands in ACT behind a copy that waits for PE's spread): 700 to 725 us. Rival (the B copies with their own waits carried it): under 695 us, and the run with B by PE is the slow one.

> The changed kernel with POOL's B brought as before: PE spreads it, ACT copies it two steps ahead, 48 times; C stays on the DMA. Theory 'C carries it': 674 to 682 us for the scans. Rival 'B carries it': 700 us or more. If the parts only add up together (this run plus the one with C by PE well under 736 in sum of their excess, 64 us), the two copies in one step are what ACT can't fit.

The scans take 707 and 738 us. Groups of the first, then of the second:

```profile
L1696 DVE TENSOR_TENSOR_SCAN mem<-mem,ps 128x1024 f32<-128x1024 f32 x144 | 335.7, 2332 | 58.7 <-issue 29.4 <-DVE ps L1682 14.6 <-ACT mem L1612 11.4
L1618 ACT COPY mem<-ps 128x1024 f32<-128x1024 f32 x192 | 194.1, 1011 | 136.4 <-PE ps L1563 122.8 <-POOL mem L1667 13.3
```

```profile
L1691 DVE TENSOR_TENSOR_SCAN mem<-mem,ps 128x1024 f32<-128x1024 f32 x144 | 335.8, 2332 | 78.8 <-issue 44.1 <-ACT mem L1607 25.9 <-DVE ps L1677 5.1
...
L1613 ACT COPY mem<-ps 128x1024 f32<-128x1024 f32 x48 | 48.6, 1012 | 155.7 <-PE ps L1557 155.7
```

B alone lengthens the scans by 66 us, with 48 copies of 1.01 us, before which ACT stands idle for 155.7 us waiting for PE. C alone brings 35, with 122.8 us of such waits. Both are more than `s5_both_and_wait` has from copies without these waits. But neither is the kernel before in part: there the two waits are 54.1 and 78.4 us. In the run with B by PE the granted clock of the scans is also only 0.83, where it was 0.94 before, and a matmul of `accumulate`, which the spread stands behind, takes 724 ns in place of 630. So what share of the 64 us was B's and what C's stays open.

Nor do the places agree, though the totals are near (736 before, 738 with B by PE). The scans run in twelve chunks of 16 states. In three of them ACT also makes the softplus of delta (in the first chunk half of one, in the last chunks of tiles 0 and 1 a whole one for the next tile). Counted from the starts of the scans, in us:

| | before | after | `s5_both_and_wait` | `s6_c_by_pe` | `s7_b_by_pe` |
|---|---|---|---|---|---|
| the three chunks with softplus | 231.6 | 191.4 | 202.8 | 210.9 | 212.5 |
| the other nine | 504.4 | 480.8 | 483.2 | 495.7 | 525.4 |

The change took 40 of its 64 us out of the three chunks, and B by PE puts 45 of its 66 into the other nine. The longest of these stops, in the kernel before:

```profile
1958.57 1.28 ACT L1317 ACT_TABLE_LOAD   x1
...
1959.87 3.71 ACT L1317 ACTIVATE mem<-mem 128x2048 f32<-128x2048 f32 x2
...
1966.12 2.35 DVE L1679 TENSOR_TENSOR_SCAN mem<-mem,ps 128x1024 f32<-128x1024 f32 x1 [8.77 <-issue]
```

ACT switches to the logarithm and back, and the next decay comes 8.77 us late for DVE; at the same place the changed kernel loses 3.17 us. A likely reading is that the copies and their waits had used up ACT's lead, so that this extra work fell on DVE in full; no run tests it.

The timeline of the run with B by PE shows the order that does it:

```profile
2013.85 1.88 PE L1566 MATMUL ps<-mem 128*128 128x512 f32 x4
...
2015.57 0.60 PE L1557 MATMUL ps<-mem 96*128 x2
...
2016.04 1.21 DVE L1677 TENSOR_TENSOR ps<-ps,mem 128x1024 f32<-128x1024 f32 x1
2016.20 1.01 ACT L1613 COPY mem<-ps 128x1024 f32<-128x1024 f32 x1 [3.52 <-PE ps L1557]
...
2017.11 1.15 ACT L1607 ACTIVATE mem<-mem 128x1024 f32 x1
...
2018.29 2.35 DVE L1691 TENSOR_TENSOR_SCAN mem<-mem,ps 128x1024 f32<-128x1024 f32 x1 [1.05 <-ACT mem L1607]
```

PE's spread of B (L1557, 2015.57) stands behind `accumulate` (L1566, 2013.85), which waits for POOL by its code; ACT's copy (L1613) follows at 2016.20, after 3.52 us in which ACT stood idle, and the decay (L1607), behind that copy in ACT's order, begins at 2017.11 and ends at 2018.26; DVE's product (2016.04, 1.21 long) has been done for 1.05 us when its scan starts at 2018.29, and the row names the decay as the releaser. In this run it is an in-order wait of ACT, and not its busy time, that delays DVE.

### Layer 3

```diff
-    NSTG = 4
+    NSTG = 2
...
-                rows(t)
+                if t:
+                    rows(t - 1)
+            rows(NT - 1)
```

> The changed kernel with two edits in layer 3: the rows of a tile follow the whole next tile again, and the conv sums have two slots again in place of four. Now 158 us pass from the last scan to PE's first patch matmul (194 before) and 34 us from PE's last one to the end (38 before), with 80 us between them (76 before). By the prediction the order of the rows carries most of the 36: 175 to 190 us to the first patch. Rival (the faster preparation of each tile carries it): 160 to 170 us. The two slots: by the prediction PE's part and the tail together grow by 0 to 12 us; rival: nothing, since ACT's copies wait for patches and not for slots.

```profile
2452.79 0.35 SPq L1822 DMA_DIRECT2D l_planes<-mem  x1
...
2488.95 55.93 SPq L1836 DMA_DIRECT2D mem<-l_planes  x28
...
2515.65 3.83 PE L1871 MATMUL ps<-mem 56*32 56x256 f16 x136 [99.22 <-DMA mem<-l_planes]
```

From the last scan to the first patch it takes 169 us, where the change has 158 and before had 194. This trace runs 3.4 us behind that of after at the end of the scans; less these, the first store (2452.79) is 14 us later than in after and the patch loads (2488.95) are 11 us later. So the order of the rows carries 11 of the 36, and the other 25 stay with the rest of the edits there (ACT's quarters in phase order, the shifted copies off POOL, the taps loaded in the norm), which weren't taken apart. In the groups of the two traces, DVE's small copies of columns fall from 40.1 to 22.8 us in sum and its subtractions from 23.7 to 14.7. The two slots: PE's part and the tail are 114.6 us, 114.0 with four and 113.9 before. The slots had no value.

## Why the prediction was wrong, and where it was right

**Layer 0, wrong.** The step that failed is the reading of the share: "while ACT waits, the DMA engines are moving the bytes it waits for: only the 0.04 left, 21 us, is idle DMA time. So transfers set this stretch." The bytes were the same in `b1_before_first`, the share rose to 0.99, and the stage fell by 97 us. A share counts the time in which a packet is under way, and the packets became shorter (904 to 749 ns for 16 KB) once the taps came in time; what makes them so, whether other kinds of transfers beside them or something else, was not taken apart. So 21 us was no limit to what earlier taps could give back, and the terms "I take 5 us back" and the bound of -35 under them were mis-sized: `e1_old_taps` puts the taps' timing at 59 us. Rival D had the mechanism ("the taps were more than a symptom") and gave 2635 for it, with a chance of 0.13; its "against", 512 us of DMA work that would have to shrink, was the same false floor. Even its 49 us for the stage were too few.

**The layout, of no account, as forecast.** -12 for windows and +9 for base stores make -3; the run with old taps has -4, too little to tell from nothing. Counted from the packets' times on 16 engines, windows went at 221 GB/s before (74 ns for 1 KB), and in 8 KB runs at 255 in `e1_old_taps` and 283 in after, so the 215 taken for them was low. The base stores went at 341 in after (48 ns for 1 KB), the near bound, as taken; rival C is out.

**The split mid-batch.** The fear of up to 2 us a batch for PE was right in kind: PE waits 18.7 us in all for the split, and `e3_head` has a stage 8 us shorter, though that is within what the stage varies by.

**Layer 2, right in size, the cause only in part.** -58 forecast, -64 measured; two thirds of 89.7 us of idle time were to go, and 63.1 went, 70%. The rates of the new loads, "246 GB/s" for 4 KB runs on 64 partitions, came as 253. But the reason given, that "ACT's copies are what makes it late" with 243 us of ACT's time, does not hold for their time: in `s5_both_and_wait` the time and POOL's wait give 14 us. With a wait for PE as in the bracket in [rows 7], 1.14 us before L1602, the copies cost 35 and 66 us. Nor was the place shown in [rows 7] typical: of the 63.1 us of idle time that went, 41.7 stood in a few long stops that the rows put down to "issue" (50.7 us in 15 stops before, 9.0 in 3 after), twelve of the fifteen in the three chunks with softplus. Rival E began to come (the clock fell from 0.94 to 0.87, `accumulate` from 630 to 691 ns) without a sign that it cost anything: PE has 180 us to spare there, and DVE's products wait 3.3 us for it, 2.4 before.

**Layer 3, right in sum.** -36 measured at PE's start against -32, and 0 against the -6 of the slots. Most of what was put on the order of the rows belongs to the rest of the edits, 25 of 36 us. The step that gave the slots a value took ACT's wait of 13.7 us for them [rows 10] as a delay; without it ACT waits for the next sum, which waits for patches.

**The range.** It took its lower end from rival D at 2635 and a little, and 2617.67 lies below it. With the false floor out of the way, nothing in the rows bounded the taps' term at 49 us.

## What to carry to other kernels

A DMA share near one says that packets are always under way, not that they go as fast as they can: compare the rate in GB/s with the best stretch of the same transfers before calling a stage bound by them. Where an engine waits for a load, look up where the load stands in its queue's program and what its issuer waits for ahead of it; moving it ahead took no memory here and was worth more than a third buffer. Of a copy in front of a critical instruction, read the wait in its bracket as well as its duration: here 192 copies of 1 us cost 7 us in all without a wait, and 35 with one for PE. And add up an engine's idle time by place before explaining it by one place: a few long stops held most of it.

## What the runs showed of the hardware

The same transfers, in packets of the same sizes, went at 263 GB/s before, 298 in `e2_old_rows` and 322 in `b1_before_first`, at shares of 0.96, 0.98 and 0.99. Loads that repeat one DRAM row of 4 KB on 64 partitions went at 253 GB/s while busy, as fast as loads of x in 4 KB runs from distinct rows ahead of layer 3 (246, [rows 3]), so the source being one row cost nothing that can be seen. By the Trainium skill, "SBUF — State Buffer", section "A bandwidth-pool intuition that's wrong (but worth ruling out)", one of 32 HBM ports gives about 22.5 GB/s; no such limit showed for these rows. Issuing three transfers from ACT kept its queue for 3.5 us in the batch shown, and the next compute instruction started right behind.
